# Blank rows and padding stored behind a step's token and triangle loads, two a step, in a post-norm decoder layer

## The reference, cut to what matters

```python
x = layernorm(x + attn(x))            # gated delta rule
x = layernorm(x + xattn(x, ctx))      # 16 heads over a context of 8 x 256 x 256
x = layernorm(x + ffn(x))             # mixture of experts
# attn: q, k, v = silu(dwconv(x @ W)); delta rule in chunks (T = inv(I - attn)); three FIR filters of v;
#       the statistics of all five paths and x go through a gate: gelu(gate_in @ gW1) @ gW2, softmax;
#       the weighed paths are summed, normed and projected by Wo
# ffn:  two shared experts, and 8 routed ones of which each token takes the best 2
```

## Time and profile before

| | us |
|---|---|
| median of 3 runs | 983.86 (983.17 to 991.73) |
| the profiled execution | 988.87 |
| its span in the profile | 987.1 |
| TensorE busy in the span | 857.3 (87%) |
| VectorE busy | 611.5 (62%) |
| ScalarE busy | 437.1 (44%) |
| blank stores | 17 of 1040 KB, median 6.8 us from issue to landing |

### The profile page before, as it was taken

One profiled execution on the slowest core, in us unless ns is written; L12 is line 12 of the kernel. 1 busy time (PEld: TensorE's weight loads), 2 busy tenths in 40 slices (PEclk: granted clock), 3 DMA queues, 4 the chain that ended last, 5 costly groups with the idle time before them and its releaser, 6 DMA issues.

```text
span 987.1 us, 18152 instructions
## 1 busy us (share of the span) xinstructions
PE 857.3 (87%) x6731; PEld 635.3 (64%) x6731; DVE 611.5 (62%) x1440; ACT 437.1 (44%) x797; POOL 343.4 (35%) x310
## 2 busy tenths in 40 slices
PE   6998779789887988877878878889997999999995
PEld 4666657667665665656555555556785777777774
DVE  5899679565887788853557776774461343333255
ACT  4787556445565464532144543445331322222221
POOL 9322110222553455632001342233540242222584
PEclk9999799777998998989799998999997999999998
DMA  5799759897969897147432222302202222221421
GB/s 164 222 265 259 203 139 267 292 228 199 236 173 262 207 224 213 60 134 237 129 106 73 95 95 78 113 24 93 86 22 83 56 63 65 65 65 49 150 65 64
DMA packets 157686, 138.73 MB, mean 141 GB/s; under 512 B 90848, under 2 KB 131744, under 8 KB 156320
## 3 DMA queue, kind: packets, MB, share of 16 engines
q1 hardware_dynamic: 154192, 128.20, 46.6%
q0 software_dynamic: 3408, 9.38, 2.5%
HBM read 82.44 MB, written 55.10 MB: 139 GB/s over the span
## 4 chain that ended last, share of the span: by engine, by line
PE 57%; DVE 17%; ACT 9%; DMA 5%; issue 4%; POOL 4%; SPq 3%; POOLq 0%; DVEq 0%; ACTq 0%
PE ps L2618 10%; PE ps L2633 5%; PE ps L2018 5%; PE ps L661 4%; DVE cross_room L2051 3%; PE ps L2482 3%; PE ps L418 2%; PE ps L2080 2%; POOL kept L2765 2%; PE ps L2495 2%; PE ps L1399 2%; DVE big L1451 2%; PE ps L2124 2%; PE ps L1407 1%; PE ps L1951 1%
## 5 line engine op out<-in xcount | busy, mean ns | idle before, releaser
L2096 ACT ACTIVATE cross_room<-ps 128x1024 f32<-128x1024 f32 x64 | 65.5, 1024 | 95.1 <-PE ps L2022 95.1
L2051 DVE TENSOR_REDUCE cross_room<-ps 128x4 f32<-128x1024 f32 x64 | 78.0, 1223 | 43.1 <-PE ps L2018 42.9
L2018 PE MATMUL ps<-kept,cross_room 32*128 32x256 f32 x512 | 75.3, 422 | 33.8 <-DVE cross_room L2051 25.5
L2618 PE MATMUL ps<-wr,xbT 128*128 x312 | 100.7, 466 | 1.8 <-ACT xbT L2654 1.8
L2707 POOL DMA_INDIRECT y_dram<-yb,dest_row x39 | 37.5, 961 | 137.5 <-DVE dest_row L2683 133.3
L2018 PEld LDWEIGHTS ps<-kept,cross_room 32*128 32x128 f32 x512 | 48.2, 196 | 50.9 <-ACT cross_room L2096 26.4
L1367 POOL TENSOR_TENSOR st<-st,exponent 128x20 f32<-128x20 f32 x16 | 56.5, 3534 | 66.6 <-DVE st L1342 65.3
L2618 PEld LDWEIGHTS ps<-wr,xbT 128*128 128x128 f32 x312 | 59.4, 191 | 30.1 <-issue 3.5
L2022 PE MATMUL ps<-cross_room,kept 32*128 32x256 f32 x512 | 75.3, 413 | 0.0
L545 DVE SCALAR_TENSOR_TENSOR room<-room 128x256 f32<-128x256 f32 x144 | 58.3, 477 | 15.2 <-ACT room L494 15.2
L2692 DVE TENSOR_TENSOR cross_room<-cross_room,ps 128x352 f32<-128x352 f32 x39 | 20.3, 521 | 60.3 <-PE ps L2618 60.3
(11 more groups left out here) (348 smaller groups left out, 2191.9 us busy)
## 6 DMA issues: line engine op xcount, KB each, us to landing
xs_dram<-staged SPq DMA_DIRECT2D x17, 1040.0 KB, 6.8
room<-in_gW SPq DMA_DIRECT2D x8, 1280.0 KB, 8.4
tok_dram<-room SPq DMA_DIRECT2D x8, 768.0 KB, 7.9
fir_dram<-room SPq DMA_DIRECT2D x6, 1024.0 KB, 7.3
paths<-fir_dram SPq DMA_DIRECT2D x48, 128.0 KB, 3.6
xb<-xs_dram SPq DMA_DIRECT2D x39, 130.0 KB, 2.4
hank<-rt_dram SPq DMA_DIRECT2D x8, 512.0 KB, 7.8
kept<-k_pad SPq DMA_DIRECT2D x8, 512.0 KB, 4.8
```

What stands on the lines that cost most here:

```text
L2018: m1 = nc.tensor.matmul(ps[:, c, t * T:(t + 1) * T], strips(qS[b % 3], g, c)[:, t * P:(t + 1) * P], kS(b, g)[c * CH:(c + 1) * CH], start=T ...
L2051: V.tensor_reduce(mx[:, :, g, XD + 2 * h * CH:XD + (2 * h + 1) * CH + 1:CH].rearrange("p t c -> p c t"), ps[:, pair(h), :].rearrange("p c ...
L2096: S.activation(pT[g % 2][:, pair(h)].rearrange("p c k t -> p (c k t)"), ps[:, pair(h), :].rearrange("p c n -> p (c n)"), ACT.Exp).then_inc ...
L2618: m = nc.tensor.matmul(ps[:, 2 * (j % 2) + half, 0:FF], xbT[j % 2][:, k, :], wr[:, bass.ds(e, 1), k, half, :].rearrange("p e n -> p (e n)" ...
```

## The change

The blank stores become one piece each, n from 0 to 16, and blanks and padding move to round 5 of their step. So in every step they stand behind the tokens and triangles, and, from step 4 on, behind the x1 store and its wait. Their number and sizes stay. The steps are now: 2 and 3 two blanks each; 4 to 7 a blank, a quarter of the padding, a blank; 8 three blanks; 9 the last two and the small one.

```diff
-        def sp_blank(step):
+        def sp_blank(n):
             sp.wait_ge(s.cleared, 6 + NCH)
-            strips = NE * STRIDE // P
             places = env.xs_dram[0:NE * STRIDE].rearrange("(p k n) w -> p k n w", p=P, n=BLANKS)
-            for k in range(step * 12, min(step * 12 + 12, strips // BLANKS), 4):
-                nc.sync.dma_start(places[:, k:k + 4], env.blank.unsqueeze(1).broadcast_to([P, 4, BLANKS, XW])).then_inc(*s.blank_out.up(16))
-                yield
-                yield
-            if step == 5:
+            nc.sync.dma_start(places[:, 4 * n:4 * n + 4], env.blank.unsqueeze(1).broadcast_to([P, 4, BLANKS, XW])).then_inc(*s.blank_out.up(16))
+            if n == NE * STRIDE // P // BLANKS // 4 - 1:
                 nc.sync.dma_start(env.xs_dram[NE * STRIDE:NE * STRIDE + P], env.blank[:, 0]).then_inc(*s.blank_out.up(16))
-            yield
...
-        C, X, out, back = sp_context, sp_x1, sp_keep_keys, sp_fetch_keys
-        sp_beside = {3 + n: sp_blank(n) for n in range(6)} | {
-                     9: rounds({0: ((C, 0), (C, 1))}),
+        C, X, out, back, fill, blank = sp_context, sp_x1, sp_keep_keys, sp_fetch_keys, sp_filling, sp_blank
+        sp_beside = {2 + n: rounds({5: ((blank, 2 * n), (blank, 2 * n + 1))}) for n in range(2)} | {
+                     4 + n: rounds({5: ((blank, 2 * n + 4), (fill, n), (blank, 2 * n + 5))}) for n in range(NCH)} | {
+                     8: rounds({5: ((blank, 12), (blank, 13), (blank, 14))}),
+                     9: rounds({0: ((C, 0), (C, 1)), 5: ((blank, 15), (blank, 16))}),
...
-        weave([sp_invert, sp_states, sp_statistics, sp_gate, sp_project_out], B, {2: sp_rest, 3: sp_cross} | {4 + c: lambda c=c: sp_filling(c) for c in range(NCH)},
+        weave([sp_invert, sp_states, sp_statistics, sp_gate, sp_project_out], B, {2: sp_rest, 3: sp_cross},
               sp_beside)
```

## The result

The changed kernel takes 993.46 us (median of 15 runs, 989.35 to 1000.67); the kernel before, timed beside it, 989.22 (median of its 15 runs by then, 978.74 to 992.2). The ratio of the comparison, which is not simply the quotient of the two medians, is 1.0114, with a 95% interval of 1.0086 to 1.0143: 11 us slower, between 8.5 and 14. The forecast was 5.7 us slower, and most of its chance lay within 1%. The direction was right. The size was half of what came out.

What follows compares the result with a forecast made beforehand. It took the delta stage to be bound by a chain through engines, with late tokens and a context load through SP's queue. Terms -3.4 + 3.2 + 5.9 = +5.7 us on 983.86 gave 989.6 us, range 981.0 to 996.4.

Steps and rivals of the forecast that it cites:

- What bounds the stage, and where transfers are on the chain: Delta stage: chain mostly through engines, except SP's queue to batch 6's tokens (TensorE idle 5.71 us) and a 3.67 us context load.
- Steps 2 to 4, nothing: Early delta steps: moved blanks delay only loads used a step later or more; no cost, or 2.8 us if cover fails.
- Step 5, the gain: Batch 6's tokens: one blank less ahead lands them sooner, 25.0 us after the x1 store; 3.4 us gained, bounds 0 and 7.8.
- My second way to count: Batch 6's tokens: issue at 304.2 plus a landing of 6.0 to 7.7 us without blanks ahead, so landed at 310.2 to 311.9.
- The bound of 7.8: Most the token gain could be: all 5.7 us of TensorE idle time gone, plus 2.1 us from the clock.
- Step 8, the first loss: The `dx_gate` load, behind padding and a second blank, lands too late for the gate's transposes; 3.2 us lost, bounds 0 and 5.7.
- Steps 9 and 10, the second loss: Behind step 9's x1 store, blanks delay the context load and ScalarE's key write, so L1407; 5.9 us lost, bounds 3 and 6.8.
- The sum: Whole kernel: -3.4 + 3.2 + 5.9 = +5.7 us, giving 989.6 us on the median, 0.6% slower.
- slower by over 1%: Whole kernel over 993.7 us; given a chance of 0.17.
- The first (the gain alone): Tokens' wait goes and nothing replaces it: -3.4 us, at best -7.8, so 980.5 (976.1); chance 0.18.
- The second (+12.5 us): SP held ahead of the paths, tokens' issue slips: gain 0, step 8 loses 5.7, tail 6.8; 996.4 us; chance 0.15.
- The third: Queue order makes no difference as DMA engines share among transfers; only ScalarE's wait is left, about +4, 987.9 us; chance 0.10.

Runs made afterwards that it cites:

- tail-alone kernel: Kernel before, with only its last two big blanks and the small one moved from step 8 to behind step 9's x1 store; ratio 1.0043.
- the second run: Changed kernel, with step 7's two blanks and padding issued ahead of its x1 store's wait; ratio 1.0064.
- own-buffer run: Changed kernel, with a separate buffer for the blank rows so ScalarE's key write needn't wait; 55.8 us from step 9's x1 store to the first score matmul.
- the two single edits: Changed kernel with either a separate blank-row buffer or step 10's context loads ahead of the last blanks; 55.8 and 56.4 us from step 9's x1 store to first score matmul.

## Why the prediction was half right

**What bounds the stage, and where transfers are on the chain:** right. The stages in which the chain goes through SP's queue were the ones that moved, and steps without such a place kept their 27.0 us.

**Steps 2 to 4, nothing:** right. From the first transposes of step 2 to those of step 5 it is 77.4 to 77.5 us in both profiles of either kernel, and step 5's transposes wait for VectorE and not for tokens in all four. From step 4's x1 store to step 5's it is 27.0 us in all fourteen profiles.

**Step 5, the gain (3.4 forecast, 2.5 measured).** The step that failed is "the queue was full all along: one blank less makes 25.0", that is, the one price of 2.8 us for a blank wherever it stands. The tokens landed 26.2 us after the x1 store, since two blanks behind the paths went, at 2.6 each, and one came ahead of them, at 3.6. The full queue was taken from the old order, and the new one doesn't fill it as well. Two windows, first of the kernel before, then of the changed one, each from step 4's x1 store to the landing of the tokens (the columns end with clock, DMA share and GB/s):

```profile
286.30:314.00 27.70, 20.20 (x239) 14.74 (x237) 23.34 (x40) 14.64 (x30) 14.92 (x10) 0.97 0.98 244
```

```profile
281.93:307.90 25.97, 20.21 (x239) 14.75 (x237) 22.29 (x38) 14.66 (x30) 13.74 (x8) 1.00 0.94 219
```

In the old order the big blanks stood behind the path loads, and from the end of the paths' issue to the landing the share was 1.00 or above. In the new one they are gone by then, SP is held in the issue of the path loads (11.93 us in place of 10.3), and the share is 0.95 from there on. That this is the whole reason for the two prices is argued from these windows, not shown by a run. My second way to count had the range for it (issue 17.9, measured 18.7; landing 6.0 to 7.7, measured 7.5), but I took the sum from the first. Of the 2.5 us gained, 1.6 are idle time where I had 2.8, and 0.9 the clock behind it where I had 0.6. The bound of 7.8 was out of reach, as 33.3 us can fall to 27.0 at the least: 6.3.

**Step 8, the first loss (3.2 forecast, 5.2 measured).** The step that failed is the sum that took the lateness of `dx_gate` alone and left TensorE's clock, some 2 us, to the bound. The wait is as described: moving this load alone gives 3.0 us back. That this is so near 3.2 is in part luck. The load was issued 18.1 us after the x1 store and landed at 21.8, where I had 17.0 and 20.7; and TensorE, which had come to these transposes 17.5 us after the store, now came at 19.2, so that it waited 2.66 us.

VectorE's waits show where the 5.2 us are, since they alone differ from x1 store to x1 store. First the kernel before, then the changed one:

```profile
382.63 0.69 DVE L1582 TENSOR_TENSOR delta_room<-ps,dx_res 128x512 f32<-128x512 f32 x1 [0.59 <-PE ps L1554]
395.08 0.69 DVE L1498 TENSOR_REDUCE so<-big 128x8 f32<-128x512 f32 x1 [0.69 <-ACT big L1443]
406.17 0.69 DVE L1582 TENSOR_TENSOR delta_room<-ps,dx_res 128x512 f32<-128x512 f32 x1 [1.95 <-PE ps L1554]
```

```profile
376.53 0.69 DVE L1577 TENSOR_TENSOR delta_room<-ps,dx_res 128x512 f32<-128x512 f32 x1 [1.38 <-PE ps L1549]
391.20 0.69 DVE L1493 TENSOR_REDUCE so<-big 128x8 f32<-128x512 f32 x1 [2.91 <-ACT big L1438]
404.49 0.69 DVE L1577 TENSOR_TENSOR delta_room<-ps,dx_res 128x512 f32<-128x512 f32 x1 [4.17 <-PE ps L1549]
```

The second is a place I hadn't named: the late transposes hold ScalarE's copy of their result, which stands ahead of the squares that VectorE's last sum needs. That is 2.2 us. With the 0.8 of the first, which come before `dx_gate` is needed, already the x1 store of step 8 is 3.0 us later (25.82 us after step 7's, before 22.82). Step 9 adds another 2.2 at the third.

The tail-alone kernel, whose `dx_gate` is in time, has 1.30, 0.70 and 3.34 us at the three places. So 2.1 us of the loss come without `dx_gate`, 0.7 in step 8 and 1.4 in step 9. In all five other kernels with `dx_gate` in time the stretch took 48.0 to 48.6 us and not 46.4. The windows from step 8's x1 store to step 9's show the part in step 9, first the kernel before, then the run with the tail alone:

```profile
396.44:419.99 23.55, 19.50 (x94) 15.26 (x92) 20.22 (x30) 12.02 (x22) 16.89 (x12) 0.97 0.20 62
```

```profile
391.50:416.45 24.95, 21.94 (x94) 17.78 (x94) 20.23 (x30) 10.90 (x18) 16.89 (x12) 0.87 0.17 54
```

VectorE does the same instructions in the same time, and TensorE's are nearly the same, but it is busy 2.4 us longer at a mean clock of 0.87 in place of 0.97. The 0.7 of step 8 seem to come from step 7: the clock was 0.94 there and not 1.00, and the profile has 261 matmuls in it and not 270. The other runs fit: with 1.00 in step 7 but 0.86 in step 9 the second run took 22.8 us for step 8, as before, and 25.2 for step 9; the own-buffer run, with 0.96 in step 9, took 24.7 there, 1.1 less than the changed kernel (0.85), though its `dx_gate` was late too. I supposed this to be chance in the first profile of before; a second gave the same 46.4. Up to step 7 the tail-only kernel has before's very order, and its clock was 0.94 there against 1.00. So it isn't the order of step 7 that makes the difference, and what does, and whether the timed runs of the kernel before always have the better clock, stays open.

**Steps 9 and 10, the second loss (5.9 forecast, 6.9 measured).** Right in place and in both causes. The context's transposes began 10.6 us after the x1 store where I had 9.5, since the context load took 6.41 us to land in a loaded queue, and L1402 began at 11.7 in place of 10.6. From there to VectorE's start behind L1549 it took 5.9 us in place of 5.2: the clock cost 0.7, and I had 1.0. So the step of the working that failed is the landing of the context load, which came 1.1 us later than I had it. That both waits end together was in the working (9.7 and 10.6), and the two single edits, which gave nothing, show that it matters.

**The sum.** +5.7 became +9.6 in the profiled stretches: 0.9 less gain, 2.0 more at step 8, 1.0 more at the tail. All three errors have one sign. The largest is the clock of steps 7 to 9, which was in the bound and at nothing in the sum. The bounds of the first two terms hold what was measured, while that of the tail, 6.8, was just passed. The chance I gave to "slower by over 1%" asked for all bounds at once; three moderate misses were enough.

**The rivals.** The first (the gain alone) is what the changed kernel is with step 7's two blanks and padding and the last three stores moved ahead of their waits, and even then the timed runs don't tell it from no change. The second (+12.5 us) came nearer to the timed 11 us than the forecast: its losses, 5.7 and 6.8, are close to the measured 5.2 and 6.9, and an extra blank delayed the tokens' issue by 3.6 us, between its 4.6 and my 2.8. But its own mark, no gain at the tokens, didn't come: they landed 1.6 us sooner. The third fell: the place of one blank made 3.6 us for the tokens.

## What to carry to other kernels

"Behind the tokens" is two places when the issuing engine then stands at a wait: ahead of that wait a filler runs in idle time, behind it it is first in line at the busiest moment. Moving the same stores across those waits was worth about 1.7% (ratios to the kernel before of 1.0114 and 0.9948, from two comparisons). Before moving a bulk store, look for what waits on its completion (here a write to a buffer that it shares), and for the shortest step among those that get the same treatment; and where two waits end together, one alone can't be priced by taking it away.

## What was not expected of the hardware

Issuing through a loaded queue is not a fixed price. Six path loads of 128 KB took SP 4.36 us to issue with only an x1 store just ahead of them, 10.12 with one blank and a quarter of the padding, 11.93 with two blanks and the padding. And about a fifth of the stage's difference, 2.1 of 9.6 us, goes with TensorE's granted clock: kernels with the same order of instructions up to there had a mean of 1.00 or 0.94 in step 7, and with nearly the same work in step 9, 0.97 or 0.87. No run here shows what sets it.
